# A fifth bank of each attention row transposed by DMA, and the row's sums added by POOL

## The reference

```python
def L0(t, x, adj, alpha, beta):
    deg = jnp.clip(adj.sum(axis=1), 1.0)
    dis = deg ** (-0.5)
    diffusion = (dis[:, None] * adj * dis[None, :]) @ x - x
    norms = jnp.maximum(jnp.linalg.norm(x, axis=-1), 1e-08)
    sim = x @ x.T / (norms[:, None] * norms[None, :])
    attn = softmax(beta * sim * adj, axis=1)
    return diffusion + sigmoid(alpha) * (attn @ x - x)
def L1(X, adj, W):
    return relu(adj @ (X @ W))
x = layernorm(x + L0(t, x, adj, alpha, beta))
x = layernorm(x + L1(x, adj, W))
```

## Time and profile before

| | us |
|---|---|
| median of 3 runs (694.83 to 694.93) | 694.9 |
| the profiled execution, by its own time | 695.17 |
| its span, first to last instruction | 693.4 |
| PE busy | 660.7 |
| DVE busy | 569.1 |
| ACT busy | 430.4 |
| POOL busy | 248.7 |

### The profile page before, as it was taken

The page is one execution under the profiler, slowest core; times in us unless marked ns, Lnnn a source line. Parts: engine busy times, 40 slices in busy tenths (PEclk is TensorE's granted clock), DMA queues, the critical chain, the costliest instruction groups (busy, mean ns, idle before and its releaser), DMA issues.

```text
span 693.4 us, 18265 instructions
## 1 busy us (share of the span) xinstructions
PE 660.7 (95%) x5651; PEld 524.8 (76%) x5651; DVE 569.1 (82%) x1684; ACT 430.4 (62%) x873; POOL 248.7 (36%) x225
## 2 busy tenths in 40 slices
PE   6868999999999999999999998699999999999997
PEld 6536777777777777777777776598888888888886
DVE  4857999999999999999999999876767676666664
ACT  5867999989898898999999997202222223111111
POOL 2699344644546455464464555600000000000000
PEclk8999999999999999999999999899999999999999
DMA  7687799999999999999999993400000000000000
GB/s 250 186 237 182 189 243 249 260 248 257 243 257 261 242 267 235 258 250 252 244 254 257 255 237 68 61 5 1 0 0 0 0 0 1 17 15 30 15 15 30
DMA packets 154532, 105.25 MB, mean 152 GB/s; under 512 B 135696, under 2 KB 136208, under 8 KB 154512
## 3 DMA queue, kind: packets, MB, share of 16 engines
q1 hardware_dynamic: 154512, 105.01, 59.5%
HBM read 69.34 MB, written 2.10 MB: 103 GB/s over the span
## 4 chain that ended last, share of the span: by engine, by line
PE 87%; DVE 5%; POOL 4%; issue 1%; ACT 1%; DMA 1%; SPq 0%; DVEq 0%; POOLq 0%; ACTq 0%
PE ps_e L1015 30%; PE ps_s L926 21%; PE ps_e L958 8%; PE ps_e L937 7%; PE ps_acc L958 7%; PE ps_e L961 4%; PE ps_acc L961 4%; PE ps_s L975 1%; PE ps_e L975 1%; DVE stage L703 1%; DMA x_keep<-in_x 1%; DVE scores L632 1%; POOL x_parts L344 1%; PE ps_at L910 1%; POOL u L359 1%
## 5 line engine op out<-in xcount | busy, mean ns | idle before, releaser
L926 PE MATMUL ps_s<-xn_parts,xn_signed 128*128 128x512 f16 x756 | 205.4, 382 | 10.3 <-POOL xn_signed L303 7.5
L632 DVE CUSTOM_DVE_ANT_1 scores<-ps_s,adj_bytes 128x512 f32<-128x512 f32 x252 | 171.5, 681 | 27.4 <-issue 14.1
L445 ACT ACTIVATE scores<-scores,col 128x1024 f32<-128x1024 f32 x128 | 157.4, 1232 | 9.5 <-DVE col L643 9.4
L326 POOL TENSOR_SCALAR e_parts<-scores 128x1024 f16<-128x1024 f32 x64 | 84.0, 1312 | 166.4 <-ACT scores L445 113.6
L413 ACT ACTIVATE adj_bytes<-land 128x1024 uint8<-128x1024 f32 x128 | 133.6, 1048 | 0.0
L1015 PE MATMUL ps_e<-x_parts,stage 128*128 128x256 f16 x1024 | 113.0, 273 | 0.0
L1015 PEld LDWEIGHTS ps_e<-x_parts,stage 128*128 128x128 fp8e4 x1024 | 100.2, 98 | 11.5
L452 ACT ACTIVATE eT_parts<-ps_e 128x512 f16<-128x512 f32 x128 | 75.8, 592 | 53.1 <-PE ps_e L937 52.5
L1015 PE MATMUL ps_e<-y_parts,stage 128*128 128x256 f16 x896 | 105.4, 273 | 0.2
L926 PEld LDWEIGHTS ps_s<-xn_parts,xn_signed 128*128 128x128 f16 x756 | 70.0, 98 | 46.8 <-POOL xn_signed L303 7.9
L653 DVE SCALAR_TENSOR_TENSOR e_parts<-scores,e_parts 128x1024 f16<-128x1024 f32 x64 | 96.0, 1499 | 0.1
(11 more groups left out here) (130 smaller groups left out, 1003.2 us busy)
## 6 DMA issues: line engine op xcount, KB each, us to landing
land<-in_adj SPq DMA_DIRECT2D x128, 512.0 KB, 4.5
x_keep<-in_x SPq DMA_DIRECT2D x4, 512.0 KB, 6.9
out<-u SPq DMA_DIRECT2D x7, 256.0 KB, 2.0
eTx<-e_parts SPq DMA_TRANSPOSE x64, 4.5
out<-u SPq DMA_DIRECT2D x1, 192.0 KB, 1.9
eT_parts<-in_L_gnn_weights SPq DMA_DIRECT2D x1, 64.0 KB, 7.9
scores<-in_L_gnn_weights SPq DMA_DIRECT2D x1, 64.0 KB, 1.8
out<-u SPq DMA_DIRECT2D x1, 64.0 KB, 1.6
```

The lines of the kernel that those rows point to most:

```text
L326: nc.gpsimd.tensor_scalar(e_parts[:, n, 0, :], scores[:, q, (n + 2) * CH:(n + 3) * CH], E_SCALE, 1.0, ALU.mult, ALU.mult).wait_op(sign_don ...
L445: nc.scalar.activation(piece, piece, ACT.Exp, bias=neg_max[q], scale=abs_beta, accum_out=csum[:, q, i:i + 1]).then_inc(exp_done, 1)
L632: nc.vector.tensor_tensor_reduce(scores[:, q, o:o + BANK].rearrange("p (k q) -> p k q", k=K), score_bank(h, r == 0 if start else False).re ...
L926: ins = nc.tensor.matmul(score_bank(h, start), xn_signed[:, q, part, :], xn_parts[:, other, o:o + BANK], start=(part == 0 and other == 0), ...
```

## The change

- TB is 3: PE transposes banks 2, 0 and 1 (TURN_ORDER), in slots 0, 2 and 4. `ps_e` gives each its own bank. The `turn_e`, `e_high` and `e_low` of a fourth bank, in slot 6, are gone.
- Bank 3 is a third DMA piece (n = 2) of 512 columns: one more `ex_high` (POOL) and `ex_low` (DVE, slot 3), and one more transposition of 128 x 1024 float16 (256 KB), called T2 below. Its target is the last quarter of `stage`, which the last stage uses only later.
- SP's order of a row is now: pieces 0 and 1 of `land`, T1, piece 2, T2, piece 3, T0 of the next row.
- EXP_ORDER is (2, 3, 1, 0), ATTEND_ORDER (2, 4, 5, 0, 6, 1, 7, 3). Bank 6, the first of T1, moves from place 5 (slot 0 of the next row) to place 4 (slot 7).
- `attn_add` leaves DVE. ACT scales both halves out of PSUM into `attn_sb` in one instruction (`attn_out`, 128 x 256, at the end of slot 3), and POOL adds the halves to the row with two instructions (128 x 128 each), ahead of its `ex_high`. The last `stage_block` of the attention stage waits for the last addition.

```diff
-    TB = 4
-    EXP_ORDER = (2, 3, 0, 1)
-    ATTEND_ORDER = (0, 4, 1, 5, 2, 6, 3, 7)
+    TB = 3
+    EXP_ORDER = (2, 3, 1, 0)
+    TURN_ORDER = (2, 0, 1)
+    ATTEND_ORDER = (2, 4, 5, 0, 6, 1, 7, 3)
+    DMA_BANKS = ((4, 5), (6, 7), (3,))
...
# SP
                     for i in range(C):
                         sp.wait_ge(cast_done, b * (K * C) + ((k - 1) * C + i + 1))
                         land_piece(b, k, i)
-                        if i == 1:
-                            turn_ex(r, q, 1)
+                        if i in (1, 2):
+                            turn_ex(r, q, i)
                     turn_ex(r + 1, 1 - q, 0)
...
# POOL
+            def attn_add(r):
+                pool.wait_ge(attn_read, r + 1)
+                nc.gpsimd.tensor_tensor(u[:, bass.ds(r, 1), :], u[:, bass.ds(r, 1), :], attn_sb[:, 0:D].unsqueeze(1),
+                                        ALU.add).wait_op(sign_done, 1, "sem-ge").then_inc(attn_half, 1)
+                pool.wait_ge(attn_half, r + 1)
+                nc.gpsimd.tensor_tensor(u[:, bass.ds(r, 1), :], u[:, bass.ds(r, 1), :], attn_sb[:, D:2 * D].unsqueeze(1),
+                                        ALU.add).wait_op(sign_done, 1, "sem-ge").then_inc(attn_added, 1)
...
                 pack(r + 1, 1)
+                attn_add(r - 1)
                 ex_high(r + 1, 1, 0)
                 ex_high(r + 1, 1, 1)
+                ex_high(r + 1, 1, 2)
...
# ACT
+            def attn_out(r, q, first=False):
+                act.wait_ge(attn_part, r * H + H)
+                act.wait_ge(total_done, 3 * r + 3)
+                if not first:
+                    act.wait_ge(attn_added, r)
+                nc.scalar.activation(attn_sb[:, :], attn_ps[q][:, 0:2 * D], ACT.Copy,
+                                     scale=gain).then_inc(attn_read, 1)
...
                 for h in range(H):
-                    if h % 2 == 0:
+                    if h in (0, 2, 4):
                         e_high(r, h // 2, start)
...
+                    if h == C - 1 and not start:
+                        attn_out(r - 1, 1 - q, second)
...
# DVE
-                    if h % 2 == 0:
+                    if h in (0, 2, 4):
                         e_low(r, h // 2)
-                    if h == 1:
-                        ex_low(r, q, 1)
+                    if h in (1, 3):
+                        ex_low(r, q, (h + 1) // 2)
-                    if h == 5 and not start:
-                        if second:
-                            dve.wait_ge(u_init, C)
-                        attn_add(r - 1, 1 - q)
```

More of the change, by code:

```diff
@@ L221, in two_layer_gnn, with ex_from @@
         stage8 = [stage[:, n, :].bitcast(F8).rearrange("p (b i k) -> p b i k", b=B, k=K) for n in range(G)]
+        ex_tiles = [[eTx[:, q, 0, :, :], eTx[:, q, 1, :, :],
+                     stage[:, G - 1, q * (BANK // 1):(q + 1) * (BANK // 1)].bitcast(F16).rearrange(
+                         "p (t i) -> p t i", i=P)] for q in range(2)]
+        ex_parts = [e_parts[:, 0:2, :, :].rearrange("p n a j -> p (n a j)").rearrange("p (a j) -> p a j", a=2),
+                    e_parts[:, 2:4, :, :].rearrange("p n a j -> p (n a j)").rearrange("p (a j) -> p a j", a=2),
+                    e_parts[:, 4, :, :]]
+        def ex_from(q, n):
+            return scores[:, q, DMA_BANKS[n][0] * BANK:(DMA_BANKS[n][-1] + 1) * BANK]
         def score_bank(h, start):
@@ L270, in _ @@
                 turn_ex(r, r % 2, 1)
+                turn_ex(r, r % 2, 2)
                 if r < R - 1:
@@ L348, in _ @@
                     ex_high(0, 0, 1, first=True)
+                    ex_high(0, 0, 2, first=True)
                 if n == 2:
@@ L353, in _ @@
             ex_high(1, 1, 1)
+            ex_high(1, 1, 2)
             pool.wait_ge(sigma_done, 1)
@@ L467, in _ @@
             exps(0, 0, 3)
+            exps(0, 0, 1)
+            cast(1, 1, 3, first=True)
             exps(0, 0, 0)
-            cast(1, 1, 3, first=True)
-            exps(0, 0, 1)
             row(0, 0, start=True)
-            row(1, 1)
+            row(1, 1, second=True)
             with act.Fori(2, R - 3, 2) as r:
@@ L625, in mask @@
                 dve.wait_ge(s_done, r * H + (h + 1))
-                if not start and h < TB:
-                    dve.wait_ge(e_turned, r * TB + (h + 1 - 2 * TB))
-                if not start and h >= TB:
-                    dve.wait_ge(ex_lo, 2 * r + (h // 2 - 1 - 4))
+                if not start and h in TURN_ORDER:
+                    dve.wait_ge(e_turned, r * TB + (TURN_ORDER.index(h) + 1 - 2 * TB))
+                if not start and h in DMA_PIECE:
+                    dve.wait_ge(ex_lo, r * X + (DMA_PIECE[h] + 1 - 2 * X))
                 dve.wait_ge(cast_done, r * C + (h // 2 + 1))
@@ L724, in y_low, with row @@
                                         y_parts[:, q * TC:(q + 1) * TC, 0, :], ALU.subtract).then_inc(y_lo, 1)
-            def row(r, q, start=False, second=False, last_two=False):
+            def row(r, q, start=False, last_two=False):
                 for h in range(H):
@@ L761, in _ @@
             row(0, 0, start=True)
-            row(1, 1, second=True)
+            row(1, 1)
             with dve.Fori(2, R - 3, 2) as r:
@@ L928, in cosines, with turn_e @@
                 ins.then_inc(s_done, 1)
-            def turn_e(r, q, b, start=False):
-                if b % 2 == 0:
+            def turn_e(r, q, n, start=False):
+                b = TURN_ORDER[n]
+                if n < 2:
                     pe.wait_ge(exp_done, r * C + (EXP_ORDER.index(b // 2) + 1))
-                if not (start and b < 2):
-                    pe.wait_ge(e_lo, r * TB + (b - 1))
-                for n in range(TH):
-                    t = TH * b + n
-                    ins = nc.tensor.transpose(ps_e[:, b % 2, n * P:(n + 1) * P], scores[:, q, t * P:(t + 1) * P],
+                if not start:
+                    pe.wait_ge(e_lo, r * TB + (n + 1 - TB))
+                for i in range(TH):
+                    t = TH * b + i
+                    ins = nc.tensor.transpose(ps_e[:, n, i * P:(i + 1) * P], scores[:, q, t * P:(t + 1) * P],
                                               ident[:, :])
```

113 lines of the change are left out of this document (59 added, 54 removed).

## The result

| | before | changed |
|---|---|---|
| median, us | 694.91 (694.83 to 695.0, 4 runs) | 715.24 (713.01 to 715.82, 4 runs) |
| profiled execution, span | 693.4 | 713.0 |
| mean row, 100 to 390 us | 12.49 | 13.04 |

The ratio is 1.0288, with a 95% interval of 1.0269 to 1.0307.

The account below looks back on a forecast made before the run. PE bounds the kernel at 12.46 us a row, with the DMA queue nearly full; the change makes the queue the bound. 695.2 + 35.1 (27 rows x 1.3) - 0.9 - 0.3 = 729.1, said as 729 us, range 690 to 745.

Parts of the forecast that it names:

- the slot a rival: Loop through T1, bank 6 read earlier: 12.57 us a row, 698 us; chance 0.10 with cycles near the present one.
- The size of T2's cost: DMA queue: T2 and the parted loads make the row 13.76 us, 1.3 more than now, over 27 rows +35.1 us.
- the signs named ahead: If right: rows of 13.5 to 14 us, DMA share at 1.0 or more, 250 to 270 GB/s, T0 issues of 4 us.
- this is its own speed, not what contention leaves: DMA queue: a 512 KB transposition takes 2.6 us at 200 GB/s, alone or as T0 in the middle of everything.
- the first rival: PE stays the bound, with transpositions at 292 GB/s: 0.45 us gained in about 28 rows, 682 us; chance 0.18 with mild form.
- the 12.2 us of the row before: DMA queue of the kernel before: transfers of one row, 2.7 + 6.5 + 3.5 less two overlaps of about 0.25.
- the parting of pieces 2 and 3: DMA queue: T2 between them adds a slow load start; 3.5 us becomes 2.0 + 1.3 + 2.0, less 0.2 overlap.
- 17% more bytes in less time: What the queue would have to take for PE to stay the bound; that rival had 0.18.
- ACT does not mind: Piece 3 of `land` waits behind T2 in SP's order; a load is used a row later, so no cost.
- The Trainium skill's rule: Transposing DMAs as fast as regular ones, 350 to 400 GB/s: transpositions 3.7 us a row, so rows of 12.0 us.
- How many rows, and the ends: 27 rows pay 1.3 us each; T2 costs nothing in the first rows; the end's about 2 us is hidden.
- the clock to the upper end of its range: Rival in attention: bunched PE waits lower the granted clock; unpriced, left to the upper end, 14.26 us cycle, 743 us.

Follow-up runs that it names:

- a_half_loads: The changed kernel with each load in SP's loop cut to its first 512 columns (256 KB in place of 512 KB): 684.5 us, ratio 0.9865.
- a_late6: The changed kernel with bank 6 read a slot later, in slot 0 of the next row, and bank 1 in slot 7: 710.8 us, ratio 1.0242.
- a_no_t2: The changed kernel with T2 replaced by a plain transfer of 4 KB on the same semaphore: 704.7 us, ratio 1.0161.
- b_early6: The kernel before with only ATTEND_ORDER changed, so bank 6 is read in slot 7 and bank 2 takes its place: 707.8 us, ratio 1.0196.
- b_spare128: The kernel before with one more transposition of 128 KB a row between pieces 2 and 3, which nobody waits for: 707.0 us, ratio 1.0168.
- a_dve_add: The changed kernel with the additions back on DVE, so the fifth bank by DMA alone: 719.6 us, ratio 1.0365.

## Why the prediction was right, and where it was off

Forecast 729 in 690 to 745, slower with a chance of 0.77; measured 715.2, slower. Point by point:

**PE.** Right: 12.01 us a row, seen in a_half_loads.

**ACT, DVE, POOL.** Right. ACT's copy took 0.46 us (0.45 was taken), an addition on POOL 0.55 and 0.46 (0.4 to 0.8), POOL's half `ex_high` 0.62, DVE's half `ex_low` 0.82 (0.75). In a_half_loads they cost a row nothing. Lines of the changed kernel by shape (busy, mean ns, idle before):

```profile
L705 DVE SCALAR_TENSOR_TENSOR e_parts<-scores,e_parts 128x512 f16<-128x512 f32 x15 | 12.3, 819 | 0.0
...
L343 POOL TENSOR_SCALAR e_parts<-scores 128x512 f16<-128x512 f32 x15 | 9.3, 620 | 27.4 <-DMA stage<-e_parts 27.4
...
L349 POOL TENSOR_TENSOR u<-u,attn_sb 128x128 f32 x15 | 8.3, 550 | 0.2
L352 POOL TENSOR_TENSOR u<-u,attn_sb 128x128 f32 x15 | 6.8, 457 | 2.4 <-POOL u L349 2.4
...
L499 ACT ACTIVATE attn_sb<-ps_e,col 128x256 f32<-128x256 f32 x8 | 3.7, 463 | 0.0
```

**Two costs with one effect.** The prediction made the queue the cause and the slot a rival that would count only if the queue were elastic. The runs show a limit of each: with the queue's load alone 13.00 us (a_late6), with the slot alone 12.99 on the old kernel and 12.75 with T2 out, with both 13.04. They do not add; the numbers are what one expects where the slower of two limits counts. The rival's mechanism was right, its condition (an elastic queue) was not needed, and its price was too low: 12.57 was said for the changed kernel, 12.75 measured in a_no_t2. The chain of a_no_t2 shows which term was short:

```profile
201.12 1.71 SPq L264
...
204.84 6.77 DMA eTx<-e_parts
...
223.56 0.34 DVE packT L676
...
224.67 1.76 DVE e_parts L709
...
226.50 2.96 SPq L264
```

From T0's issue to T1's landing are 10.5 us (10.7 were said), then PE for 11.9 (12.0), and then DVE for 2.9 up to the next issue, where 2.4 was said: between the last cosines and `ex_low` DVE has `store_adj` and others of its row as well. In b_early6 the same three are 10.3, 11.9 and 3.9 us (issues at 214.79 and 240.88).

**The size of T2's cost.** This is the term that was mis-sized: 13.76 us were taken for the row, 13.04 measured, 0.72 x 27 = 19 us. The measured row lies inside the 12.8 to 14.3 us that had the largest chance. Of the signs named ahead, rows of 13.5 to 14 us did not come; the DMA share over 1, the 260 GB/s and SP's 3.2 to 4.3 us for T0 did. Where the 0.72 lies is seen when the packets of the trace are cut at each change between transposed and loaded bytes (means of 21 rows between 110 and 392 us, in us; standing still counts to the loads, and these 21 rows are 0.1 us longer than the mean row above):

| | T0 | pieces 0, 1 | T1 | pieces 2, 3 (and T2) | sum |
|---|---|---|---|---|---|
| before | 2.53 | 3.65 | 2.82 | 3.47 | 12.48 |
| changed | 2.27 | 3.42 | 2.69 | 1.86 + 1.64 + 1.26 = 4.76 | 13.14 |

The last stretch grew by 1.3 us, as much as the sum had said, though not by its terms: piece 3 took 1.26 in place of 2.0, T2 1.64 in place of 1.3. What the sum had left as it was, T0, the first two loads and T1, shrank by 0.6 together.

Two steps failed. First, "this is its own speed, not what contention leaves", of a transposition at 200 GB/s. That holds for one that is issued into an empty queue: in b_early6, where every T0 is, it flows for 2.58 to 2.60 us in 21 rows of 21. The prediction took the row with such a T0 for all rows. In the changed kernel T0 is issued while piece 3 still drains, and takes 1.84 to 2.81 us. The fastest, fully issued by 221.85 (SP's rows above), flows at 288 to 290 GB/s (last column):

```profile
221.50:222.00 0.50, 0.50 (x4) 0.22 (x3) 0.50 (x1) 0.30 (x1) 0.42 (x2) 1.00 1.28 288
222.00:222.50 0.50, 0.50 (x7) 0.40 (x5) 0.50 (x1) 0.50 (x2) 0.50 (x1) 1.00 1.27 290
222.50:223.00 0.50, 0.50 (x8) 0.36 (x5) 0.50 (x2) 0.50 (x1) 0.50 (x1) 1.00 1.27 289
```

That is the rate the first rival had read from the microsecond 206 to 207 in the earlier trace rows, and only the rival was given it. The fuller queue moved more per us, so the 12.2 us of the row before were not a floor to which T2 adds its lone duration: the mixed rate went from 252 to 260 GB/s. Second, the sum costed the parting of pieces 2 and 3 by a new start, 0.5 less 0.2. With 256 KB in the gap the runs give nothing for it (12.98 between, 13.04 behind); with 128 KB they give 0.44 (12.92 against 12.48). Why the start hides behind the larger one alone stays open; a possible reason, not tested, is that only the larger one lasts as long as the next load needs to begin.

**The rival's bytes.** "17% more bytes in less time" is a slip: 3.41 MB in place of 3.15 are 8% more. For PE's 12.01 us that asks for 284 GB/s, and the fullest stretch of 260 us here has 263.

**ACT and the late load.** "ACT does not mind" that piece 3 comes behind T2: so in the changed kernel, but not in a_late6, where ACT waits for a load 15 times in 200 us, 7.8 us in all. It was not tested what that costs.

**The Trainium skill's rule.** The page "Advanced Engine Details and Errata" of the Trainium skill, section "X-Bar Transpose (TRN2)", has transpositions as fast as other DMAs, 350 to 400 GB/s. No stretch here shows that: a transposition has 200 lone and up to 290 queued, the mix 260 to 263. The page "DMA: Bandwidth & Descriptors" of the Trainium skill, section "Latency and other measured facts", gives 261 GB/s for a transposition whose middle dimension isn't contiguous; the mix here has the same number, but more than half of its bytes are plain loads, so this is no confirmation.

**How many rows, and the ends.** 27 rows x 0.55 = 14.9 us. The last load comes 20.6 us later than before (426.78 against 406.20), and what follows it is as long as before (286.2 against 287.2 to the end of the span). So some 5.7 us were lost in the first rows, which the prediction had at nothing. It offsets part of the 19 us above, so 729 came nearer to 715 than its row did to the measured row; that is luck. By the second `turn_adj` the changed kernel is 1.6 us late (73.4 us in place of 71.9). That is what one wait at 65 us grew by: PE waited 3.7 us for the signed copy of x, in place of 2.1 (why POOL is later there was not tested):

```profile
PE ps_s L963 <- POOL xn_signed L320: 3.7, 1, 3.7
```

Another part is a row of 15.84 us: PE waited 1.94 us for T1, and for the three us behind it the granted clock was 0.61, part of it at 1.2 GHz:

```profile
98.27 0.28 PE L996 MATMUL ps_e<-x_parts,eTx 128*128 128x256 f16 x1 [1.94 <-DMA eTx<-e_parts]
```

The window behind it (clock, DMA share and GB/s last):

```profile
98.00:101.00 3.00, 2.73 (x15) 1.98 (x16) 0.29 (x1) 0.62 (x2) 1.05 (x1) 0.61 0.95 226
```

The prediction had left the clock to the upper end of its range without a price. Here the row is 2.8 us over the mean. The clock has some 1.7 of them, by an estimate: 0.61 over these 3 us and 0.82 over the next 3 are 1.2 + 0.5 us short of full speed. The rest is the wait. The end was as forecast: the last `stage_block` is hidden.

## What to carry to other kernels

Read how full a shared queue is (bytes per row over its mixed rate) before giving it more; here 252 of 262 GB/s were in use, and room for 128 KB stood against a need of 256. When work is moved to a slower path, look at the circle its result closes: one bank moved in an order table, with no byte and no instruction more, cost 13.6 us. And to know what the rest of a change is worth, halve the resource under suspicion: a_half_loads told in one run that all other parts are free when the queue has room, though not which of two limits through that queue had held the row. Read a rate from several rows: the one T0 that the prediction read was of the slower kind.

## What the hardware showed that was not expected

- A transposing DMA of 512 KB from SBUF to SBUF flows at 200 GB/s when it is issued into an empty queue (2.6 us, in 21 of 21 rows of b_early6). Issued behind loads that still drain, it took 1.84 to 2.81 us in the changed kernel, and the fastest ran at 288 to 290 GB/s.
- Loads and transpositions in one queue, mixed about 3 to 2 by bytes, ran at 260 to 263 GB/s in the six kernels here that load the queue most, with different orders. The DMA share doesn't tell this by itself: it is 1.06 or 1.07 as well in b_spare128 and a_dve_add, at 254 and 256 GB/s.
- A transposition of 128 KB between two loads cost 12.8 us over 28 rows, behind them nothing that can be told; one of 256 KB cost 13.6 and 15.8. Size and place do not act apart.
